# A recurrent mixing layer on one core: two small products as unpadded row tiles, and every engine's order written out anew

## The reference

```python
xn = ln(x)                                   # layer norm over the features
sx = token_shift(xn, prev)                   # previous token minus this one
t  = tanh((xn + sx * maa_x) @ maa_w1)        # 5 x 32 values for a token
x5 = xn + sx * (maa_stack + t.reshape(5, 32) @ maa_w2)   # five mixes: k, w, v, r, g
w  = exp(-exp(time_decay + tanh(x5[1] @ decay_w1) @ decay_w2))
r, k, v = x5[3] @ Wr.T, x5[0] @ Wk.T, x5[2] @ Wv.T
g  = silu(x5[4] @ Wg.T)
# along the tokens, state s of 8 x 8 for each head:
out_t = r_t . (u * k_t v_t + s);   s = k_t v_t + w_t * s
x  = x + (groupnorm(out) * g) @ Wo.T
# then a second layer norm, token shift, and
x  = x + sigmoid(xr @ Fr.T) * (relu(xk @ Fk.T)**2 @ Fv.T)
```

## Time and profile before

| | |
|---|---|
| median of 3 runs | 521.76 us |
| profiled execution | span 520.3 us from the first to the last instruction; the three runs lie from 520.23 to 522.25 |
| TensorE | 479.2 us busy, 92% |
| VectorE | 474.4 us busy, 91% |
| ScalarE | 281.7 us, 54% |
| GpSimd | 101.6 us, 20% |
| DMA | 134 GB/s mean |

### The profile page before, as it was taken

One profiled execution on the slowest core, in us unless ns is written; L12 is line 12 of the kernel. 1 busy time (PEld: TensorE's weight loads), 2 busy tenths in 40 slices (PEclk: granted clock), 3 DMA queues, 4 the chain that ended last, 5 costly groups with the idle time before them and its releaser, 6 DMA issues. The chain is left out here.

```text
span 520.3 us, 6254 instructions
## 1 busy us (share of the span) xinstructions
PE 479.2 (92%) x2200; PEld 284.2 (55%) x2200; DVE 474.4 (91%) x528; ACT 281.7 (54%) x612; POOL 101.6 (20%) x93
## 2 busy tenths in 40 slices
PE   4868889997989999999999999999999999979896
PEld 2555545553456455655556365655555566556475
DVE  2688899979999999999999989999999999999765
ACT  2443575477537664567645844666636552527243
POOL 0001001301331124210430033211531032122020
PEclk9978999999999999999999989999999999999999
DMA  8282473697389616991489435990579439542030
GB/s 265 121 231 52 107 166 85 145 217 151 72 204 230 122 26 167 220 217 19 103 219 242 85 81 139 216 201 1 121 189 220 78 61 227 126 72 71 1 41 30
DMA packets 26999, 69.49 MB, mean 134 GB/s; under 512 B 1624, under 2 KB 19928, under 8 KB 24536
## 3 DMA queue, kind: packets, MB, share of 16 engines
q1 hardware_dynamic: 19720, 54.68, 41.4%
q0 software_dynamic: 7248, 14.42, 16.4%
HBM read 46.28 MB, written 12.19 MB: 112 GB/s over the span
## 5 line engine op out<-in xcount | busy, mean ns | idle before, releaser
L630 DVE TENSOR_TENSOR_SCAN kv<-w_sb,kv 128x512 f32<-128x512 f32 (+2 forms) x144 | 146.6, 1084 | 0.1
L958 PE MATMUL pa<-x,large_sb 128*128 128x512 f32 (+2 forms) x272 | 115.2, 567 | 5.0 <-DVE x L545 2.9
L451 POOL COPY kv<-s_sb 128x32 f32<-128x32 f32 (+2 forms) x36 | 54.6, 1518 | 145.6 <-PE patt L1130 141.4
L958 PEld LDWEIGHTS pa<-x,large_sb 128*128 128x128 f32 x272 | 51.2, 194 | 57.5 <-issue 44.3
L620 DVE TENSOR_TENSOR kv<-vrep,k_sb 128x2016 f32<-128x2016 f32 (+2 forms) x34 | 70.1, 2064 | 3.3 <-issue 3.3
L638 DVE TENSOR_TENSOR kv<-kv,r_sb 128x2048 f32<-128x2048 f32 (+2 forms) x36 | 72.9, 2043 | 0.2
L536 DVE SCALAR_TENSOR_TENSOR x<-pb,vec_sb,sx 128x512 f32<-128x512 f32 (+1 forms) x64 | 42.7, 708 | 6.0 <-PE pb L1002 5.9
L420 POOL DMA_DIRECT2D x<-xn x21 | 20.0, 951 | 111.5 <-DVE x L536 111.5
L1130 PE MATMUL patt<-kv,const_sb 128*32 128x512 f32 (+2 forms) x288 | 34.7, 557 | 0.5 <-DVE kv L638 0.4
L1002 PE MATMUL pb<-th,w_sb 32*128 32x512 f32 (+2 forms) x100 | 33.3, 596 | 1.5 <-DVE x L536 1.5
L1156 PE MATMUL pc<-large_sb,att 128*128 128x256 f32 x120 | 32.0, 390 | 0.0
(11 more groups left out here) (185 smaller groups left out, 824.6 us busy)
## 6 DMA issues: line engine op xcount, KB each, us to landing
vrep<-v_scratch SPq DMA_DIRECT2D x12, 2048.0 KB, 18.5
x<-xn POOLq DMA_DIRECT2D x18, 512.0 KB, 8.3
vrep<-v_scratch SPq DMA_DIRECT2D x4, 1536.0 KB, 10.8
x_tok<-in_x SPq DMA_DIRECT2D x6, 512.0 KB, 10.2
v_scratch<-v_sb SPq DMA_DIRECT2D x12, 256.0 KB
xres<-in_x SPq DMA_DIRECT2D x6, 512.0 KB, 10.7
out<-xres SPq DMA_DIRECT2D x6, 512.0 KB, 5.0
out<-trr POOLq DMA_DIRECT2D x6, 512.0 KB, 8.1
```

The source lines that it names most:

```text
L451: pool.tensor_copy(kv[:, q % 2, :, 0:nb, 0], s0_sb[:, half, G4 * j:G4 * (j + 1), FIRST[c]:FIRST[c] + nb]).then_inc(s0_put, 1)
L630: ins = dve.tensor_tensor_scan(flat, w_sb[:, p, q % HF, 0:nb].rearrange("p b t -> p (b t)"), flat, 0.0, ALU.mult, ALU.add)
L958: ins = pe.matmul(dst[:, m, 0:n], w(a)[:, m * P:(m + 1) * P], src[:, a, :], start=(a == 0), stop=(a == HF - 1))
```

## The change

The fifth mix's LoRA now folds the tokens in two instead of four: `W1` gives 32 columns on 64 PSUM partitions, and `X4` is four matmuls of 32 rows, fold f in rows 32f on, which write PSUM bank f. `D2` is four matmuls of 64 rows, fold f in rows 64f on and into bank f. The zero padding of both weights is gone (the loads are 128 KB each, from 512 and 256 KB). `mix4` on VectorE and the first exponential of `w` on ScalarE read the two banks side by side. The lists of all five engines are written out from the first step to the last.

```diff
-FOLD, DFOLD = P // LORA, P // DECAY
+FOLD, DFOLD = 2, P // DECAY
 HF = E // P
...
-DVE_ORDER = [("a3", 3), ("sc2", 3), ("sc3", 3), ("rs2", 3), ("rs3", 3), ("rk", 2), ("out", 4), ("a0", 2),
...
+DVE_STEPS = """
+    st1.0 nrm1.0 shift.0 cwv.0 mix0.0 mix1.0 mix2.0 mix3.0 cs0.0 a0.0 a1.0 sc0.0 mix4.0 shift.1 rk.0 rs0.0 sc1.0
...
-LAGS = 6
...
-def schedule(head, table, tail):
-
-    return head + [(name, i - lag) for i in range(NCH + LAGS) for name, lag in table
-                   if 0 <= i - lag < NCH and (name, i - lag) not in head + tail] + tail
+def schedule(text):
+
+    return [(name, int(c)) for name, c in (step.split(".") for step in text.split())]
...
         w1_sb = sb("w1_sb", [P, HF, 5 * LORA])
-        w2_sb, w24_sb = sb("w2_sb", [P, E]), sb("w24_sb", [P, FOLD, E])
+        w2_sb, w24_sb = sb("w2_sb", [P, E]), sb("w24_sb", [P, E])
         dw1_sb = sb("dw1_sb", [P, HF, DECAY])
-        dw2_sb = sb("dw2_sb", [P, DFOLD, E])
+        dw2_sb = sb("dw2_sb", [P, E])
         large_sb = sb("large_sb", [P, len(LARGE), HF, E])
...
+        def by_fold(ap):
+
+            return ap.rearrange("p (f t) -> p f t", f=2)
+
         def by_seq(ap):
...
             def load_v(c, p, half):
-                if half == 0:
-                    sp.wait_ge(v_stored, 16 * JH * (c + 1))
+                sp.wait_ge(v_stored, 16 * JH * (c + 1))
                 if c >= 1:
...
             sp.dma_start(w2_sb[:, :], w2[:, 0]).then_inc(in_w2, 16)
-            sp.dma_start(w24_sb[:, :, :], w2[:, 1:]).then_inc(in_w2, 16)
+            sp.dma_start(w24_sb[:, :], w2[:, 1]).then_inc(in_w2, 16)
             for names, done in LARGE_PARTS[0:2]:
             sp.dma_start(dw1_sb[:, :, :], dw1).then_inc(in_dw, 16)
-            sp.dma_start(dw2_sb[:, :, :], dw2).then_inc(in_dw, 16)
+            sp.dma_start(dw2_sb[:, :], dw2).then_inc(in_dw, 16)
             sp.dma_start(to_rows, rows_in).then_inc(in_spread, 16)
...
                 "lr": load_res, "sx2": store_x2}
-            for name, c in schedule(SP_HEAD, SP_ORDER, SP_TAIL):
+            for name, c in schedule(SP_STEPS):
                 stages[name](c, c % 2)
...
                 **{f"s0{q}": (lambda c, q=q: put_s0(c, q)) for q in range(NQ)}}
-            for name, c in schedule(POOL_HEAD, POOL_ORDER, POOL_TAIL):
+            for name, c in schedule(POOL_STEPS):
                 stages[name](c)
...
+            def mix_folds(c, n, a):
+
+                g, nt = MIXES[n], extent(c)[1]
+                nf = nt // FOLD
+                return dve.scalar_tensor_tensor(out=by_fold(x5[:, x5_slot(n), a, 0:nt]), in0=pb[:, :, a * nf:(a + 1) * nf],
+                                                scalar=vec(f"maa{g}", a), in1=by_fold(shifted(c)[:, a, 0:nt]), op0=ALU.add, op1=ALU.mult)
+
             def add_xn(c, n):
...
                 for a in range(HF):
-                    ins = mix_half(c, n, a, src[:, a])
+                    ins = mix_folds(c, n, a) if n == 4 else mix_half(c, n, a, src[:, a])
                 ins.then_inc(mixed_by(c, n), 1)
...
                 "gate": c_gate, "st2": c_moments, "nrm2": c_norm, "shift2": c_shift, "out": c_out}
-            for name, c in schedule(DVE_HEAD, DVE_ORDER, DVE_TAIL):
+            for name, c in schedule(DVE_STEPS):
                 stages[name](c, c % 2)
...
                 act.activation(th[:, 0, 0:n], pb[:, 0, 0:n], ACT.Tanh)
-                act.activation(th[:, 1, 0:n // FOLD], pb[:, 1, 0:n // FOLD], ACT.Tanh).then_inc(th_ready, 1)
+                act.activation(th[0:FOLD * LORA, 1, 0:n // FOLD], pb[0:FOLD * LORA, 1, 0:n // FOLD], ACT.Tanh).then_inc(th_ready, 1)
...
                 nb, n = extent(c)[0:2]
-                for a in range(HF):
-                    ins = act.activation(e_buf[:, a, 0:n], acc(c, pc, pb)[:, a, 0:n], ACT.Exp, bias=vec("time_decay", a))
+                nf = n // DFOLD
+                for a in range(HF):
+                    ins = act.activation(by_fold(e_buf[:, a, 0:n]), acc(c, pc, pb)[:, :, a * nf:(a + 1) * nf], ACT.Exp, bias=vec("time_decay", a))
                 ins.then_inc(e_ready, 1)
...
                 "sq": c_sq, "rstd": c_rstd, "nrm2": c_norm, "xn2": c_xn, "rr": c_rr, "kk": c_kk}
-            for name, c in schedule(ACT_HEAD, ACT_ORDER, ACT_TAIL):
+            for name, c in schedule(ACT_STEPS):
                 stages[name](c, c % 2)
...
-                        ins = pe.matmul(pb[:, a, f * nf:(f + 1) * nf], w24_sb[:, f, a * P:(a + 1) * P], th[:, 1, 0:nf],
+                        rows = slice(f * LORA, (f + 1) * LORA)
+                        ins = pe.matmul(pb[:, f, a * nf:(a + 1) * nf], w24_sb[rows, a * P:(a + 1) * P], th[rows, 1, 0:nf],
                                         start=True, stop=True)
...
                     for f in range(DFOLD):
-                        ins = pe.matmul(acc(c, pc, pb)[:, m, f * nf:(f + 1) * nf], dw2_sb[:, f, m * P:(m + 1) * P], thd[:, 0:nf],
+                        rows = slice(f * DECAY, (f + 1) * DECAY)
+                        ins = pe.matmul(acc(c, pc, pb)[:, f, m * nf:(m + 1) * nf], dw2_sb[rows, m * P:(m + 1) * P], thd[rows, 0:nf],
                                         start=True, stop=True)
...
                 "BO": bonus_in, "VR": var, "WO": wo, "T2": t2, "RR": rr, "KK": kk, "Y2": y2}
-            for name, c in schedule(PE_HEAD, PE_ORDER, PE_TAIL):
+            for name, c in schedule(PE_STEPS):
                 stages[name](c, c % 2)
...
     w1 = w["maa_w1"]
-    w2 = np.zeros((P, 1 + FOLD, E), np.float32)
-    w2[:, 0] = w["maa_w2"][0:4].reshape(P, E)
-    for f in range(FOLD):
-        w2[LORA * f:LORA * (f + 1), 1 + f] = w["maa_w2"][4]
-    dw2 = np.zeros((P, DFOLD, E), np.float32)
-    for f in range(DFOLD):
-        dw2[DECAY * f:DECAY * (f + 1), f] = w["decay_w2"]
+    w2 = np.stack([w["maa_w2"][0:4].reshape(P, E), np.tile(w["maa_w2"][4], (P // LORA, 1))], axis=1)
+    dw2 = np.tile(w["decay_w2"], (DFOLD, 1))
     mats = {"Wr": w["Wr"].T, "Wk": w["Wk"].T, "Wv": dh(w["Wv"].T), "Wg": dh(w["Wg"].T), "Wo": dh(w["Wo"]).T,
```

85 lines of the change are left out of this document (50 added, 35 removed), and 20 rows, old and new, of tables (ACT_HEAD, DVE_HEAD, PE_HEAD, POOL_HEAD).

## The result

The forecast of 515.0 us was wrong in its sign. The changed kernel takes 528.35 us as the median of 4 runs (526.49 to 532.00), beside 522.0 for the kernel before on the same chip: the ratio is 1.0133, interval 1.0091 to 1.0176. Ratios are of fast runs alone, which lie within 1.5% of the fastest of their kernel, and medians are of all runs. The profiled execution took 527.61 us with a span of 525.8, so I explain +5.5 us of span where I had forecast -6.8.

A forecast was written before the change was run, and what follows sets the result against it. VectorE's 474.4 us of work was taken as the floor. 520.3 - 6.0 (start) - 2.8 (middle) + 2.0 (end) = 513.5 us span, median 1.5 above: 515.0; range 511 to 519 (chance 0.50), wider range 508 to 521.5.

The forecast's parts named there:

- VectorE's work unchanged: Whole kernel: VectorE's busy time stays at 474.4 us, its instructions being unchanged in number and size.
- TensorE in a chunk: Each full chunk: `X4` -0.8 us, `D2` -0.75, `W1` +0.5, so TensorE has 1.05 us less to do.
- Rival D: 64-row or 32-row tiles do not run side by side, TensorE becomes the bound: median 521.3 us; chance 0.21 with rival A.
- The first 60 us: Start: VectorE waits of 7.4 us go, against 0.5 for `W1` and 0.9 for small new waits: -6.0 us.
- Chunk 2: VectorE's wait for v's copy at `a0.2`, 2.72 us before, gets no better: 3.0 taken, bounds 1 and 5.
- rival A: Early gain lost at `a0.2`, whose wait for v's copy grows to 8.7 us: median 521.5; chance 0.21 with Rival D.
- The rest of the middle: Up to 460 us, without `a0.2`: VectorE's 2.21 us wait falls to 1.1, seven others from 4.0 to 2.0.
- The end: Tail: `a3.8` and `sc3.8` ahead of `shift2.7` start `RR.7` 2.6 us later; +2.0 us taken, between 0 and +2.6.
- Rival C: TensorE's clock drops to 1.2 GHz once in each of chunks 2 to 8, costing 15.5: median 529.5; 0.11 with similar mishaps.

The follow-up runs named there:

- e1_tiles: The changed kernel with all five engines' orders put back to those of the kernel before, so new tiles alone: 520.85 us, ratio 0.9970 to the kernel before.
- e14_graft_pad: The orders of e10_graft with the old padded tiles, FOLD of 4 and one bank: 512.24 us, ratio 0.9800 to the kernel before.
- after: The changed kernel itself, with new tiles and new orders, against the kernel before: 528.35 us, ratio 1.0133.
- e6_p02: The changed kernel with `P0.2` moved ahead of `BO.1` and `S0.1` on TensorE: 522.06 us, ratio 0.9979 to the kernel before.
- e9_p02_tail: The changed kernel with the edits of e5_tail and e6_p02 together: 518.65 us, ratio 0.9925 to the kernel before.
- e10_graft: New tiles, new orders up to chunk 2 with `P0.2` ahead of `BO.1`, then the old orders: 513.89 us, ratio 0.9836 to the kernel before.
- e5_tail: The changed kernel with the last steps of VectorE, TensorE and ScalarE in the old order: 525.24 us, ratio 1.0042 to the kernel before.
- e12_again: The changed kernel, unchanged, measured a second time: 527.73 us, ratio 1.0121 to the kernel before.
- e13_adwait: The changed kernel with the DMA add `ad3.2` waiting until v's store of chunk 2 has landed: 534.68 us, ratio 1.0239 to the kernel before.
- e7_sp: The changed kernel with the old order of the DMA queue SP: 537.94 us, ratio 1.0280 to the kernel before.

## Why the prediction was wrong, step by step

**VectorE's work unchanged.** Right: 473.3 us for 474.4.

**TensorE in a chunk.** Right to 0.1 us. `X4` and `D2` take 1.13 us, the 64-row tiles run side by side, and the thin part of `W1` takes 1.06, +0.4 for the 0.5 assumed. Rival D, as far as it was about the tiles, is out. That this would be worth something was a smaller term of the sum, and it turned out at 0.3% (`e1_tiles`), or at nothing (`e14_graft_pad`).

**The first 60 us.** Right in mechanism and size. `cwv` is hidden (the wait before the first mix is 4.06 us), no wait over 1 us is left between 20 and 50 us, and VectorE idles 14.3 us there. `rk.1` starts at 60.87; in the kernel before its row reads:

```profile
68.03 0.95 DVE L589 TENSOR_TENSOR th<-r_sb,k_sb 128x768 f32<-128x768 f32 x1
```

That is 7.2 us of lead (6.2 to 8.3 in the other traces with this head), 6.0 forecast.

**Chunk 2: the first step that failed.** The prediction said of `a0.2`: "Bounds 1 and 5 us; I take 3.0", and added the start's 6.0 in full. That priced the wait as if v's copy would come earlier by as much as everything else. It came later than that. The wait was 6.1 to 6.7 us in four of the five traces with these lists, and of the lead 2.6 to 5.1 us were left at `a0.2`, for the 5.7 forecast. In the trace of `after` it was 4.00 and nearly all of the lead was gone: `a0.1` waits 3.35 us for v, `bonus.1` behind it holds `W1.2`, which then runs at the lower clock (3.58 us, 1.95 where the clock is full), and `P0.2` stands behind `BO.1` and `S0.1`, so that `v.2` starts at 90.47 us, before at 90.44. TensorE's timeline after has the two slow products:

```profile
70.58 3.58 PE L995 MATMUL pb<-mix,w_sb 128*128 128x512 f32 x4 [2.95 <-DVE bonus L600]
...
103.54 5.40 PE L963 MATMUL pa<-x,large_sb 128*128 128x512 f32 x8 [2.38 <-DMA x<-xn]
```

This is rival A, to which I gave with D 0.21; it had the right place and one right reason ("`P0.2` is moved back"), but its size, all of the lead, is that of the one trace. It did not have the other reason: under the new lists `ad3.2` goes out 2.0 to 2.5 us behind v's store, and the store then takes 11.3 to 12.2 us. Two things in my own rows spoke for it: `a0.2` was already the longest wait of the middle, and I had counted the 2.3 us by which `P0.2` is late. `e6_p02`, `e9_p02_tail` and `e10_graft` show the mend: with `P0.2` ahead in the new lists the lead reaches `a0.2` at 110 us, and with the old lists behind it the end.

**The rest of the middle: the second.** The forecast for it was -3.1 us (the -2.8 without the 0.3 for `a0.2`); measured from `a0.2` to `a0.8` are -0.7 in this trace and +1.8 to +3.6 in the four others. The waits for the first LoRA products mostly went here (0.47 us left, 3.90 before), but new ones for v came: 0.81 at 228.83 for the first half of chunk 4, and 2.21 at 356.73 for the second half of chunk 6 (2.4 to 3.6 in the others), whose `vl1` now stands behind the residual's load. I had not followed SP's queue past chunk 2. What the rest of the loss in the others is, I did not separate.

**The end: the third, and the one that every trace shows.** Forecast +2.0, measured +6.5 (counted from `a0.8`), and +6.2 to +7.3 in the other traces that have this tail. I had looked at `shift2.7` and its place, and counted the scans ahead of `gate.7` as a gain (-0.88, a wait that goes). `gate.7` is what `WO.7` waits for; TensorE stood idle for 4.32 us (4.8 to 5.3 in the others) and lost its clock. `S1.8` ahead of `T2.7` was the second thing that I passed over. The missed waits are TensorE's, not VectorE's. Mended (`e5_tail`), the tail takes 42.1 us for the old 40.1, so the +2.0 for `shift2.7`'s place was not needed to explain what is left, and I can't say what it was worth.

**The clock.** Rival C named the lower clock as a danger in the middle, in seven chunks. The granted clock there is 0.99. It fell at `W1.2`, at `P3.2` and in the tail, each time behind a wait of TensorE that the orders made. In `e12_again` `W1.2` and `P3.2` kept the full clock, and the time was the same, so the loss does not need these two.

Sum of this trace: -0.3 up to `a0.2` (forecast -5.7), -0.7 to `a0.8` (-3.1), +6.5 to `Y2.7` (+2.0), 0 behind it: +5.5. The same sum for `e12_again`: -4.2, +1.8, +7.3, 0: +4.9. The total repeats, the tail repeats; how the rest divides between chunk 2 and the middle does not.

## What to carry to other kernels

A lead that one engine wins at the start is worth something only if the next step that everything waits for starts earlier too; find the first transfer on the way and follow what produces it, instruction by instruction, before adding the gain to the sum. When steps are moved ahead of another, look first at who waits for the step that is passed (`gate.7`, `P0.2`, `T2.7`), and not at the waits that go. A change made of good and bad parts should be tried place by place: here the new lists up to chunk 2, with one step put back and the old lists behind them, are 1.6% faster than before, the whole 1.3% slower. And one trace is one run: the first one read here put the whole lead's loss into chunk 2, and four more traces with the same lists up to there kept 2.6 to 5.1 us of it past chunk 2.

## What was not expected of the hardware

- v's store took 8.7 us with no add issued in its first 4 us, and 12.2 us when a DMA add of 0.5 MB was issued 2.0 us behind it; 2.3 us more distance took all of the 3.5 us away. The add issued 0.55 us behind a load of 2 MB was waited for until 13.4 us after its issue (`e13_adwait`), where its median is 6.4.
- TensorE's clock behind waits of like length is not always the same. Behind a wait of 3.8 us `WO.7` kept the full clock in `e5_tail` (5.3 us) and lost it in `e9_p02_tail` (6.8 us, granted clock 0.60 from 458 to 462), and `W1.2` took 1.96 us behind a wait of 2.38 (`e13_adwait`) but 2.85 behind one of 2.01 (`e7_sp`). The first rows of `WO.7`, `e5_tail` and then `e9_p02_tail`:

```profile
465.58 0.70 PE L1161 MATMUL pc<-xres,const_sb 128*128 128x256 f32 x2 [3.81 <-DVE att L658]
```

```profile
458.04 1.22 PE L1161 MATMUL pc<-xres,const_sb 128*128 128x256 f32 x2 [3.82 <-DVE att L658]
```

- Ten warming matmuls in a wait of 4.32 us kept the clock and took 2.7 us off `WO.7`, without one step moved; by medians the kernel gained 2.6 us, in intervals that overlap.
